# Self-attention on one Trainium2 core: five key tiles a step summed by accumulating transfers, one on TensorE, the narrow matmuls of a step in 9 blocks

## The chip, the cores and the metric

The kernel runs on one core of one Trainium2 chip. Its engines work side by side and are tied only by semaphores: TensorE (PE), VectorE (DVE), ScalarE (ACT), GpSimd (POOL) and SyncE (SP), which here only issues transfers. GpSimd issues transfers too, on a queue of its own. The metric is the device time of one execution in microseconds, lower is better.

## The reference

The program is a chain of transformer layers in fp32 on x of shape (2, 2048, 512): adaptive layer norm and cross attention, then a block with self-attention, cross attention and an mlp. The change touches only the self-attention, 16 heads of 32 channels over 2048 keys:

```python
def mha(q, k, v):
    B, Nq, C = q.shape
    d = C // H
    ...
    scores = jnp.einsum('bqhd,bkhd->bhqk', qh, kh) / jnp.sqrt(jnp.asarray(d, q.dtype))
    attn = jax.nn.softmax(scores, axis=-1)
    out = jnp.einsum('bhqk,bkhd->bqhd', attn, vh)
    return out.reshape(B, Nq, C)
...
qkv = h @ qkv_w + qkv_b
q, k, v = jnp.split(qkv, 3, axis=-1)
h = mha(q, k, v) @ self_o_w + self_o_b
```

## The kernel before

The stages follow one another: conditioning, a cross pass, a dense pass that makes q, k and v, `attention`, a second cross pass, and `mlp`. Each ends before the next begins.

`attention` makes 32 steps (`STEPS`): 2 batches, 4 groups of 4 heads (`GH`), 4 chunks of 512 queries (`W`). A step has for its 512 queries and 4 heads:

- 64 **score tiles** (`score_tile`, L1844), one for each of 16 key tiles and 4 heads: keys on the partitions, queries in the free dimension, into one of three PSUM banks `st`. ScalarE turns each into exponentials `e` (`exponential`, L1959). `e` has five slots (`ER`) of one key tile with its 4 heads, so key tile t+5 can be written only when all readers of tile t are done.
- 64 **peak units** (`score_unit`, L1822), the same scores with the queries on the partitions, into one of three banks `sm`. VectorE takes their largest value (`peak_of_unit`, L2003). They belong to the next step and the one after: the peaks must be known before a step's score tiles, since their negative is a row of q. `HEAD` = 21 says how many units of a step are done two steps ahead. When a step's 64 are done, VectorE makes `minus` (L2012, L2013), GpSimd the low part (`lower_parts`, L2077), TensorE turns them (`turn_peaks`, L1832) behind score tile `TURN` - 1 = 48, ScalarE copies them to `rows` (L1947), and SP spreads them into q by a transfer (`spread_rows`, L1763), which must be there before the next step's score tile 0.
- 16 **products** with v (`weigh`, L1857), 4 matmuls of 32 columns each into `acc[:, 0]`.
- The **sums of the exponentials** over the 16 key tiles, into `acc[:, 1]`. Ten tiles (`POOLED`) are added up by GpSimd into `esum` (`add`, L2070, nine adds). Four (`MOVED`) are summed by transfers that GpSimd issues into `esum_moved` (`move`): the first a copy (L2091), the others accumulating (L2094), each waiting for the one before it to land. Two (`SUMMED`) are multiplied by ones on TensorE (`add_up`, L1866). At the end `add_moved` (L1882) and `add_partial` (L1875) multiply `esum_moved` and `esum` by ones into the same sums.

A *unit* of narrow matmuls is what one call of `weigh`, `add_up`, `add_moved` or `add_partial` issues: four matmuls of 32 columns, eight in the records. A step has 20. TensorE's order is written out by hand: it goes through x = 0 to 63, and for each x issues score tile x, then the narrow units that `products` lists for x, then peak unit x. The narrow units stand in 11 *blocks*, at x = 0, 5, 10, 16, 22, 27, 33, 39, 44, 53, 59; the last units of a step come in the first blocks of the next. A score tile waits for the exponential that frees its bank (`bank_free`), three places back, and two back at the edge of a step, because a step has 65 places (64 tiles and the transposes). A peak unit waits for the peak three units back.

ScalarE copies `acc` out behind exponential `FETCH_AT` = 10 of the next step (`fetch_sums`, L1973). VectorE divides in three parts at units `DIVIDE_AT` (L2023, L2027, L2034), ScalarE spreads the inverse at `SPREAD_AT` = 42 (L1966), GpSimd scales (`scale`, L2083), and SP stores (L1772).

GpSimd's order within a step is also written out: move 0 before add 1, move 1 before add 3, move 2 and `lower_parts` before add 6, move 3 before add 8, `scale` before add 9. SP's order is: q for two steps ahead once score tile 63 of the step before is done (L1745, three transfers), in every fourth step k (L1753, three of 1 MB), then a wait for the sums of the step before and v (L1757), then the store, then the spread.

Of the kernel before, what the change touches and what calls it, by code (L numbers as in the profile page):

```python
# [16 lines left out]
HEADS, DH = 16, 32  # L17
# [1596 lines left out]
def attention(nc, d, name, q_in, k_in, v_in, o_out, keys, preload):  # L1614
# [10 lines left out]
    NKT = -(-keys // P)  # L1625
    KR = keys // NKT
# [9 lines left out]
    QR = 3  # L1636
    ER = 5

    POOLED = [0, 1, 3, 5, 7, 8, 9, 11, 13, 14]
    MOVED = [2, 6, 10, 12]  # L1640
    SUMMED = [4, 15]
    SUMMED_FIRST = [4, 15]
    ADDS = max(len(POOLED) - 1, 0)
    STEPS = B * GROUPS * CHUNKS
    BODY = STEPS
    TURN = 49
    HEAD = 21
    TILES = GH * NKT + 1
    RING = 3
    LATE = 1 if NKT > 1 else 2  # L1650
    DIVIDE_AT = (13, 23, 57)
    FETCH_AT, SPREAD_AT = 10, 42
    SETUP = 2 + KW % 2
    with nc.cleanup_on_exit(), ExitStack() as ctx:
        sb = lambda n, s, t=F32: ctx.enter_context(nc.sbuf_tensor(f"{name}_{n}", s, t))
# [3 lines left out]
        acc = ctx.enter_context(nc.psum_tensor(name + "_acc", [P, 2, W], F32))  # L1659
        ident = sb("ident", [P, P])  # L1660
        mask = sb("mask", [P, GH])
        ones = sb("ones", [P, DH])
# [4 lines left out]
        if POOLED:  # L1667
            esum = sb("esum", [P, GH, W])
            esum_moved = sb("esum_moved", [P, GH, W])
# [17 lines left out]
        e_moved, esum_read = sem("e_moved"), sem("esum_read")  # L1687
# [6 lines left out]
        def exists(i, j):  # L1694

            return not isinstance(i, int) or 0 <= BODY * i + j < STEPS
# [112 lines left out]
        def _(pe):  # L1809
# [61 lines left out]
            def add_partial(i, j):  # L1871

                pe.wait_ge(e_added, (BODY * i + j + 1) * ADDS)
                for h in range(GH):
                    mm = pe.matmul(acc[h * DH:(h + 1) * DH, 1], ones[0:KR], esum[:, h], start=False, stop=True, tile_position=(0, h * DH))  # L1875
                mm.then_inc(tile_used, 1)

            def add_moved(i, j):

                pe.wait_ge(e_moved, DMA * (BODY * i + j + 1) * len(MOVED))  # L1880
                for h in range(GH):
                    mm = pe.matmul(acc[h * DH:(h + 1) * DH, 1], ones[0:KR], esum_moved[:, h], start=False, stop=False, tile_position=(0, h * DH))  # L1882

            def products(i, j, x):

                if x == 0 and exists(i, j - 1):
                    weigh(i, j - 1, 13)
                    add_up(i, j - 1, 15)
                elif x == 5 and exists(i, j - 1):
                    weigh(i, j - 1, 14)  # L1890
                    weigh(i, j - 1, 15)
                elif x == 10 and exists(i, j - 1):
                    add_moved(i, j - 1)
                    add_partial(i, j - 1)
                elif x == 16 and exists(i, j):
                    weigh(i, j, 0)
                    weigh(i, j, 1)
                elif x == 22 and exists(i, j):
                    weigh(i, j, 2)
                elif x == 27 and exists(i, j):  # L1900
                    weigh(i, j, 3)
                    add_up(i, j, 4)
                elif x == 33 and exists(i, j):
                    weigh(i, j, 4)
                elif x == 39 and exists(i, j):
                    weigh(i, j, 5)
                    weigh(i, j, 6)
                elif x == 44 and exists(i, j):
                    weigh(i, j, 7)
                    weigh(i, j, 8)  # L1910
                    weigh(i, j, 9)
                elif x == 53 and exists(i, j):
                    weigh(i, j, 10)
                elif x == 59 and exists(i, j):
                    weigh(i, j, 11)
                    weigh(i, j, 12)

            def step(i, j):
                units = units_of_step(i, j)
# [140 lines left out]
        @block.gpsimd  # L2060
        def _(pool):
            def add(i, j, x):

                n, slot = BODY * i + j, lambda x: (j * NKT + POOLED[x]) % ER
                pool.wait_ge(score_read, number(i, j, place(POOLED[x], GH - 1)) + 3)
                if x > 1:
                    pool.wait_ge(e_added, n * ADDS + x - 1)
                elif exists(i, j - 1):
                    pool.wait_ge(tile_used, n * NKT + ER)
                pool.tensor_tensor(esum[:], e[:, slot(0)] if x == 1 else esum[:], e[:, slot(x)], ALU.add).then_inc(e_added, 1)  # L2070

            def lower_parts(i, j):

                n = BODY * i + j
                pool.wait_ge(neg_hi_ready, n + 1)
                pool.wait_ge(minus_ready, n + 1)
                pool.tensor_tensor(neg_part(1).bitcast(F32), minus[:], neg_part(0).bitcast(F32), ALU.subtract).then_inc(neg_lo_ready, 1)  # L2077

            def scale(i, j):
                n = BODY * i + j  # L2080
                pool.wait_ge(o_stored[j % 2], DMA * (BODY // 2 * i + j // 2 + 1))
                pool.wait_ge(divided, DIVIDES * (n + 1))
                pool.tensor_tensor(o[:, j % 2], sums[:, 0], inv_t[:, j % 2], ALU.mult).then_inc(scaled, 1)  # L2083

            def move(i, j, y):

                n, kt = BODY * i + j, MOVED[y]
                pool.wait_ge(score_read, number(i, j, place(kt, GH - 1)) + 3)
                if y == 0:
                    pool.wait_ge(tile_used, n * NKT + ER)  # L2090
                    pool.dma_start(esum_moved[:], e[:, (j * NKT + kt) % ER]).then_inc(e_moved, DMA)  # L2091
                else:
                    pool.wait_ge(e_moved, DMA * (n * len(MOVED) + y))
                    pool.dma_start(esum_moved[:], e[:, (j * NKT + kt) % ER], accum_op=ALU.add).then_inc(e_moved, DMA)  # L2094

            def step(i, j):
                for x in range(1, len(POOLED)):
                    if x == 1 and exists(i, j):
                        move(i, j, 0)
                    if x == 3 and exists(i, j):  # L2100
                        move(i, j, 1)
                    if x == 6 and exists(i, j):
                        move(i, j, 2)
                    if x == 8 and exists(i, j):
                        move(i, j, 3)
                    if x == 9 and exists(i, j - LATE):
                        scale(i, j - LATE)
                    if x == 6 and exists(i, j + 1):
                        lower_parts(i, j + 1)
                    if exists(i, j):  # L2110
                        add(i, j, x)

            pool.sem_inc(scaled, 2)
            pool.wait_ge(small_in, 2 * DMA)
            pool.tensor_copy(k[3 * DH:P, 1], mask[3 * DH:P].unsqueeze(2).to_broadcast([DH, GH, KC * KE])).then_inc(pool_set_up, 1)
            pool.wait_ge(pool_set_up, 1)
            lower_parts(0, 0)
            run(pool, step, LATE, LATE)


# [238 lines left out]
```

## Time and profile before

| | us |
|---|---|
| median of 3 runs | 4002.65 |
| lowest and highest | 3992.6, 4006.91 |
| the profiled execution, its own time | 4006.39 |
| its span in the trace | 4004.6 |
| attention: start of the first and of the last step | 945.2, 2587.7 |
| attention: last copy of the sums | 2649.0 |

The span is what the trace covers; the execution's own time is 1.8 us more. In a row of the timeline the first number is the start, the second the duration of the merged instructions, and x8 says how many they are; in brackets stands the idle time of the engine before them and what ended it. A matmul's recorded duration is longer than the distance to the next one, since they are pipelined: distances between starts are the measure.

### The profile page before, as it was taken

The numbers are of one execution on the slowest core, as the hardware profiler recorded it, in microseconds if no ns is written. First come the engines' busy times: TensorE is split into PE (matmuls) and PEld (weight loads), VectorE is DVE, ScalarE is ACT, GpSimd is POOL, SyncE is SP. The second block draws the span as 40 slices with busy tenths as digits, with TensorE's granted clock in tenths as the row PEclk, the third lists the DMA queues.
The fourth block names the chain that finished last, engine by engine and source line by source line (L and its number), as shares of the span: only waits on it lengthen the run. The fifth ranks groups of instructions, "written<-read, shape, count | busy, mean of one in ns | idle before, by whom it ended". The sixth has DMA issues, their size and how long they took to land. (4 is left out here: it accounts for less than half of the span.)

```text
span 4004.6 us, 50633 instructions
## 1 busy us (share of the span) xinstructions
PE 3667.1 (92%) x18828; PEld 2414.8 (60%) x18828; DVE 2261.2 (56%) x3958; ACT 1862.3 (47%) x3439; POOL 2175.1 (54%) x1075
## 2 busy tenths in 40 slices
PE   4799969979999999999999999958999959999998
PEld 2577748855555445454545455427777737888887
DVE  2466642228777777777777777515665634222222
ACT  1465651113666666666666666644665521111111
POOL 0356630004888888888888888864777542000000
PEclk8798889987999999999999999978999879999999
DMA  7566556764464645556464644444576551111110
GB/s 230 146 160 168 166 159 218 222 185 105 98 143 103 149 108 127 124 110 137 101 145 106 153 101 111 120 123 111 153 179 172 134 200 42 42 42 42 42 42 31
DMA packets 231940, 505.60 MB, mean 126 GB/s; under 512 B 38151, under 2 KB 55047, under 8 KB 211751
## 3 DMA queue, kind: packets, MB, share of 16 engines
q1 hardware_dynamic: 213287, 368.49, 33.6%
q0 software_dynamic: 18432, 134.23, 15.4%
q8 instruction: 131, 2.15, 0.2%
q14 instruction: 90, 0.74, 0.1%
HBM read 215.54 MB, written 144.51 MB: 90 GB/s over the span
## 5 line engine op out<-in xcount | busy, mean ns | idle before, releaser
L2003 DVE TENSOR_REDUCE a_peak<-a_sm 128x1 f32<-128x512 f32 x2048 | 1263.3, 680 | 396.0 <-PE a_sm L1822 394.7
L1959 ACT ACTIVATE a_e<-a_st 128x512 f32<-128x512 f32 x2048 | 1061.6, 604 | 539.1 <-PE a_st L1844 506.5
L2070 POOL TENSOR_TENSOR a_esum<-a_esum,a_e 128x2048 f32<-128x2048 f32 x256 | 1210.2, 4727 | 18.8 <-POOL a_esum L2070 0.4
L1822 PE MATMUL a_sm<-a_k,a_q 96*128 96x512 f32 x2048 | 883.9, 439 | 27.9 <-DMA a_k<-s_k 27.9
L1844 PE MATMUL a_st<-a_q,a_k 128*128 128x512 f32 x2048 | 827.2, 406 | 17.4 <-ACT a_e L1959 17.2
L1822 PEld LDWEIGHTS a_sm<-a_k,a_q 96*128 96x128 f32 x2048 | 394.8, 193 | 475.8 <-DVE a_peak L2003 337.5
L1857 PE MATMUL a_acc<-a_e,a_v 128*32 128x512 f32 x4096 | 505.7, 600 | 0.0
L1844 PEld LDWEIGHTS a_st<-a_q,a_k 128*128 128x128 f32 x2048 | 387.9, 190 | 137.3 <-ACT a_e L1959 62.8
L2220 PE MATMUL mlp_ph<-mlp_us,mlp_w_hi 128*128 128x512 f32 x1024 | 336.4, 391 | 33.0 <-DVE mlp_raw_lo L2269 33.0
L2262 ACT ACTIVATE mlp_gelu<-mlp_ph,mlp_b 128x512 f32<-128x512 f32 x128 | 88.1, 688 | 595.1 <-PE mlp_ph L2220 595.1
L2277 DVE CAST mlp_gs<-mlp_gelu 128x512 fp32r<-128x512 f32 x128 | 90.8, 709 | 459.0 <-ACT mlp_gelu L2262 459.0
L2300 POOL TENSOR_TENSOR mlp_x<-mlp_x,mlp_brow 128x2048 f32<-128x2048 f32 x8 | 36.9, 4616 | 569.7 <-DMA mlp_x<-s_x 569.4
L2235 PE MATMUL mlp_py<-mlp_w_hi,mlp_gs 128*128 128x512 f32 x1024 | 317.6, 391 | 16.9 <-DVE mlp_gs L2279 16.9
L1433 POOL TENSOR_TENSOR p_e<-p_e,p_inv 128x308 f32<-128x308 f32 x256 | 173.2, 708 | 175.5 <-DVE p_inv L1109 175.4
L2220 PEld LDWEIGHTS mlp_ph<-mlp_us,mlp_w_hi 128*128 128x128 f32 x1024 | 193.5, 189 | 73.7 <-issue 33.4
L1857 PEld LDWEIGHTS a_acc<-a_e,a_v 128*32 128x32 f32 x4096 | 100.4, 108 | 219.6 <-ACT a_e L1959 124.7
L2235 PEld LDWEIGHTS mlp_py<-mlp_w_hi,mlp_gs 128*128 128x128 f32 x1024 | 191.8, 188 | 61.3 <-issue 16.3
L589 PE MATMUL p_sm<-p_ks,p_qs 96*128 96x78 f32 x1024 | 171.5, 310 | 51.0 <-DMA p_qs<-s_q 30.1
L589 PEld LDWEIGHTS p_sm<-p_ks,p_qs 96*128 96x128 f32 x1024 | 157.1, 222 | 82.8 <-DMA p_qs<-s_q 28.3
L2220 PE MATMUL mlp_ph<-mlp_us,mlp_raw_lo 128*128 128x512 f32 x512 | 200.1, 391 | 0.0
L2235 PE MATMUL mlp_py<-mlp_raw_lo,mlp_gs 128*128 128x512 f32 x512 | 199.9, 390 | 0.0
L1094 DVE TENSOR_REDUCE p_top<-p_sm 128x4 f32<-128x308 f32 x256 | 118.4, 465 | 142.5 <-PE p_sm L589 140.5
(155 smaller groups left out, 5255.1 us busy)
## 6 DMA issues: line engine op xcount, KB each, us to landing
a_esum_moved<-a_e POOLq DMA_DIRECT2D x128, 1024.0 KB, 7.3
p_qs<-s_q SPq DMA_DIRECT2D x192, 256.0 KB, 5.7
s_q<-p_qo SPq DMA_DIRECT2D x64, 512.0 KB, 7.2
a_q<-s_q SPq DMA_DIRECT2D x96, 256.0 KB, 6.8
a_k<-s_k SPq DMA_DIRECT2D x24, 1024.0 KB, 15.7
s_x<-p_x SPq DMA_DIRECT2D x16, 1024.0 KB, 4.4
s_u<-p_ut_hi SPq DMA_DIRECT2D x64, 256.0 KB, 5.8
s_u<-p_ut_lo SPq DMA_DIRECT2D x64, 256.0 KB, 6.3
```

What stands on the lines that cost most here:

```text
L589: mm = pe.matmul(sm[:, unit % 2, h * KE:(h + 1) * KE], qs[0:3 * DH, g % 2, h, qt * P:(qt + 1) * P], ks[0:3 * DH, b, g * GH + h], start=Tru ...
L1094: dve.tensor_reduce(top[:, unit % 4], src, AX.X, ALU.max).then_inc(top_done, 1)
L1433: pool.tensor_tensor(e[:, number % 2, qt, :, 0:S], e[:, number % 2, qt, :, 0:S], inv[:, number % 2, qt].unsqueeze(2).to_broadcast([P, GH, ...
L1822: mm = pe.matmul(sm[:, bank_of_unit(j, u), x * KE:(x + 1) * KE], q[0:3 * DH, j % QR, h, qt * P:(qt + 1) * P], k[0:3 * DH, g % 2, h, kc * K ...
L1844: pe.matmul(st[0:KR, place(kt, h) % RING], k[:, g % 2, h, kt * P:kt * P + KR], q[:, j % QR, h], start=True, stop=True).then_inc(score_done, 1)
L1857: mm = pe.matmul(acc[rows, 0], v[0:KR, g % 2, kt, rows], e[0:KR, (j * NKT + kt) % ER, h], start=(kt == 0), stop=(kt == NKT - 1), tile_posi ...
L1959: act.activation(e[0:KR, (j * NKT + kt) % ER, h], st[0:KR, place(kt, h) % RING], ACT.Exp, scale=SCALE).then_inc(score_read, 1)
L2003: dve.tensor_reduce(dst, src, AX.X, ALU.max).then_inc(unit_read, 1)
L2070: pool.tensor_tensor(esum[:], e[:, slot(0)] if x == 1 else esum[:], e[:, slot(x)], ALU.add).then_inc(e_added, 1)
L2220: mm = pe.matmul(ph[:, m % 4], w1[pw][:, t, m * P:(m + 1) * P], us[:, b, pm, t], start=(t == 0 and s == 0), stop=(t == KT - 1 and s == 2))
L2235: mm = pe.matmul(py[:, tt], gs[:, m % 2, pw, tt * P:(tt + 1) * P], w2[pm][:, m], start=(m == 0 and s == 0), stop=(m == HT - 1 and s == 2))
L2277: dve.tensor_copy(gs[:, m % 2, 0], gelu[:, m % 2]).then_inc(g_hi, 1)
```

## The change

The tiles are shared out anew: ten on GpSimd as before, but others, five instead of four by transfers, and one instead of two on TensorE. A step has 19 narrow units in 9 blocks, at x = 6, 10, 15, 20, 28, 34, 42, 49, 63. `add_partial` comes before `add_moved`, which now stands at x = 15 and closes the sums; a new semaphore count (`esum_read`) tells GpSimd when `esum` has been read, so that its first add of a step waits for `add_partial` alone, and move 0, now behind add 1, waits for `add_moved`. `add_up` of tile 15 stands in the block at x = 63 of the same step. `TURN`, `HEAD`, `DIVIDE_AT`, `FETCH_AT`, `SPREAD_AT` and the places of the moves and of `lower_parts` among the adds are set anew.

```diff
-    POOLED = [0, 1, 3, 5, 7, 8, 9, 11, 13, 14]
-    MOVED = [2, 6, 10, 12]
-    SUMMED = [4, 15]
-    SUMMED_FIRST = [4, 15]
+    POOLED = [0, 1, 3, 4, 6, 7, 9, 10, 12, 13]
+    MOVED = [2, 5, 8, 11, 14]
+    SUMMED = [15]
+    SUMMED_FIRST = [15]
...
-    TURN = 49
-    HEAD = 21
+    TURN = 54
+    HEAD = 16
...
-    DIVIDE_AT = (13, 23, 57)
-    FETCH_AT, SPREAD_AT = 10, 42
+    DIVIDE_AT = (26, 36, 61)
+    FETCH_AT, SPREAD_AT = 15, 40
...
 # add_partial
-                    mm = pe.matmul(acc[h * DH:(h + 1) * DH, 1], ones[0:KR], esum[:, h], start=False, stop=True, tile_position=(0, h * DH))
-                mm.then_inc(tile_used, 1)
+                    mm = pe.matmul(acc[h * DH:(h + 1) * DH, 1], ones[0:KR], esum[:, h], start=False, stop=False, tile_position=(0, h * DH))
+                mm.then_inc(esum_read, 1)
 # add_moved
-                    mm = pe.matmul(acc[h * DH:(h + 1) * DH, 1], ones[0:KR], esum_moved[:, h], start=False, stop=False, tile_position=(0, h * DH))
+                    mm = pe.matmul(acc[h * DH:(h + 1) * DH, 1], ones[0:KR], esum_moved[:, h], start=False, stop=True, tile_position=(0, h * DH))
+                mm.then_inc(tile_used, 1)
 # products
-                if x == 0 and exists(i, j - 1):
-                    weigh(i, j - 1, 13)
-                    add_up(i, j - 1, 15)
-                elif x == 5 and exists(i, j - 1):
+                if x == 6 and exists(i, j - 1):
                     weigh(i, j - 1, 14)
+                elif x == 10 and exists(i, j - 1):
+                    add_partial(i, j - 1)
                     weigh(i, j - 1, 15)
-                elif x == 10 and exists(i, j - 1):
+                elif x == 15 and exists(i, j - 1):
                     add_moved(i, j - 1)
-                    add_partial(i, j - 1)
-                elif x == 16 and exists(i, j):
+                elif x == 20 and exists(i, j):
                     weigh(i, j, 0)
                     weigh(i, j, 1)
-                elif x == 22 and exists(i, j):
+                elif x == 28 and exists(i, j):
                     weigh(i, j, 2)
-                elif x == 27 and exists(i, j):
                     weigh(i, j, 3)
-                    add_up(i, j, 4)
-                elif x == 33 and exists(i, j):
                     weigh(i, j, 4)
-                elif x == 39 and exists(i, j):
+                elif x == 34 and exists(i, j):
                     weigh(i, j, 5)
+                elif x == 42 and exists(i, j):
                     weigh(i, j, 6)
-                elif x == 44 and exists(i, j):
                     weigh(i, j, 7)
+                elif x == 49 and exists(i, j):
                     weigh(i, j, 8)
                     weigh(i, j, 9)
-                elif x == 53 and exists(i, j):
                     weigh(i, j, 10)
-                elif x == 59 and exists(i, j):
+                elif x == 63 and exists(i, j):
                     weigh(i, j, 11)
+                    add_up(i, j, 15)
                     weigh(i, j, 12)
+                    weigh(i, j, 13)
...
 # GpSimd: add
                 elif exists(i, j - 1):
-                    pool.wait_ge(tile_used, n * NKT + ER)
+                    pool.wait_ge(esum_read, n)
...
 # GpSimd: step
                 for x in range(1, len(POOLED)):
-                    if x == 1 and exists(i, j):
+                    if x == 2 and exists(i, j):
                         move(i, j, 0)
-                    if x == 3 and exists(i, j):
+                    if x == 4 and exists(i, j):
                         move(i, j, 1)
                     if x == 6 and exists(i, j):
                         move(i, j, 2)
                     if x == 8 and exists(i, j):
                         move(i, j, 3)
+                    if x == 9 and exists(i, j):
+                        move(i, j, 4)
                     if x == 9 and exists(i, j - LATE):
                         scale(i, j - LATE)
-                    if x == 6 and exists(i, j + 1):
+                    if x == 7 and exists(i, j + 1):
                         lower_parts(i, j + 1)
```

## Rows read from the trace of the kernel before

**Rows 1.** the page: the span, and GpSimd's DMA queue (packets, MB, share)

```profile
span 4004.6 us, 50633 instructions
...
q0 software_dynamic: 18432, 134.23, 15.4%
```

**Rows 2.** a stretch: us; PE, PEld, DVE, ACT, POOL busy; TensorE's clock; DMA share, GB/s

```profile
1207.00:1841.00 634.00, 626.13 (x3475) 317.12 (x3476) 487.56 (x821) 417.13 (x798) 544.85 (x179) 1.00 0.56 124
```

**Rows 3.** timeline of TensorE, one step

```profile
2130.86 0.40 PE L1844 MATMUL a_st<-a_q,a_k 128*128 128x512 f32 x1
...
2131.44 0.39 PE L1844 MATMUL a_st<-a_q,a_k 128*128 128x512 f32 x1
...
2133.09 0.40 PE L1844 MATMUL a_st<-a_q,a_k 128*128 128x512 f32 x1
...
2133.56 0.40 PE L1844 MATMUL a_st<-a_q,a_k 128*128 128x512 f32 x1
...
2148.58 0.39 PE L1844 MATMUL a_st<-a_q,a_k 128*128 128x512 f32 x1
...
2148.90 2.78 PE L1857 MATMUL a_acc<-a_e,a_v 128*32 128x512 f32 x24
...
2151.95 0.40 PE L1844 MATMUL a_st<-a_q,a_k 128*128 128x512 f32 x1
...
2156.38 0.40 PE L1844 MATMUL a_st<-a_q,a_k 128*128 128x512 f32 x1
...
2164.46 0.40 PE L1844 MATMUL a_st<-a_q,a_k 128*128 128x512 f32 x1
...
2165.28 0.47 PE L1844 MATMUL a_st<-a_q,a_k 128*128 128x512 f32 x1 [0.19 <-ACT a_e L1959]
...
2218.02 0.47 PE L1844 MATMUL a_st<-a_q,a_k 128*128 128x512 f32 x1 [0.19 <-ACT a_e L1959]
```

**Rows 4.** timeline of VectorE, the run of nine units

```profile
2152.15 5.47 DVE L2003 TENSOR_REDUCE a_peak<-a_sm 128x1 f32<-128x512 f32 x9 [1.73 <-PE a_sm L1822]
```

**Rows 5.** timeline of GpSimd, one step

```profile
2126.18 4.61 POOL L2070 TENSOR_TENSOR a_esum<-a_e 128x2048 f32<-128x2048 f32 x1
...
2136.43 0.88 POOL L2094 DMA_DIRECT2D a_esum_moved<-a_e  x1 [0.91 <-ACT a_e L1959]
...
2137.06 14.35 POOL L2070 TENSOR_TENSOR a_esum<-a_esum,a_e 128x2048 f32<-128x2048 f32 x3
...
2151.36 0.84 POOL L2094 DMA_DIRECT2D a_esum_moved<-a_e  x1
...
2168.10 4.85 POOL L2070 TENSOR_TENSOR a_esum<-a_esum,a_e 128x2048 f32<-128x2048 f32 x1
```

**Rows 6.** the accumulating transfers (L2094), issue to landing

```profile
DMA to landing us min/median/max: 6.9/7.5/9.7
```

**Rows 7.** DMA queues, 2163 to 2168 us: packets, MB, share

```profile
q0 software_dynamic: 124, 1.02, 113.0%
...
a_q<-s_q SPq DMA_DIRECT2D x3, 256.0 KB, 6.6
```

**Rows 8.** the spread of the rows (L1763), the one at 2155

```profile
L1763 SPq DMA_DIRECT2D a_q<-a_rows x1: 605/605/605, 2155.1 to 2155.1; - x1
...
DMA to landing us min/median/max: 4.8/4.8/4.8
```

**Rows 9.** timeline of TensorE, tile 0 around a load step

```profile
2005.02 0.47 PE L1844 MATMUL a_st<-a_q,a_k 128*128 128x512 f32 x1 [0.19 <-ACT a_e L1959]
...
2059.71 0.47 PE L1844 MATMUL a_st<-a_q,a_k 128*128 128x512 f32 x1 [0.19 <-ACT a_e L1959]
```

**Rows 10.** DMA issues from 2017 us on: KB each, us to landing

```profile
a_esum_moved<-a_e POOLq DMA_DIRECT2D x1, 1024.0 KB, 13.6
```

**Rows 11.** DMA queues, 2018 to 2024 us, the load step

```profile
q1 hardware_dynamic: 175, 1.30, 103.3%
```

**Rows 12.** timeline of ScalarE in the load step

```profile
2031.64 3.04 ACT L1959 ACTIVATE a_e<-a_st 128x512 f32<-128x512 f32 x6 [3.04 <-DMA a_esum_moved<-a_e]
```

## Prediction

> **What bounds the kernel now.** The page gives the span, 4004.6 us [rows 1], and names the mlp as the end of its chain; the change touches only the attention stage, so I read that stage. The table by stretches shows it: in 634 us TensorE is busy for 626, VectorE for 488, ScalarE for 417, GpSimd for 545, at a granted clock of 1.00, which is the 2.4 GHz level [rows 2]. TensorE is therefore the bound, GpSimd the next, and what matters is how TensorE's own order of work is paced. That is read from its timeline. I measure from the start of one score matmul (L1844) to the next; position x of a step is its score tile x, and I call 0 the start of tile 0 of a step.
>
> [Rows 3] give: a step takes 2218.02-2165.28 = 52.74 us. A plain pair (score tile, peak unit) takes 0.47 (2133.09 to 2133.56). A gap with a one-unit block of narrow matmuls in it takes 1.65 (2131.44 to 2133.09), with three units 3.37 (2148.58 to 2151.95), so a unit is 0.86, and a block costs 0.32 beside its units and the pair. Two-unit gaps are then 2.51, four-unit gaps 4.23.
>
> Now the sum of a step before: 53 plain gaps x 0.47 = 24.9, three one-unit blocks, seven two-unit, one three-unit: 25.9. Together 50.8; the other 1.9 us are waits. Three of them can be seen. In a run of six units between blocks the last gap is 0.58 and not 0.47 (2130.86 to 2131.44): +0.11. In the run of nine (x=44 to 53) the eight gaps 2151.95 to 2156.38 take 4.43 and not 3.76: +0.67, of which the transposes are a part. At the step's edge tile 63 to tile 0 takes 0.82: +0.35, ended by ScalarE, because 65 places a step are not a multiple of three banks and tile 0 needs the exponential of tile 62. Five runs of six, the nine and the edge make 1.6; 0.35 stays spread over small waits.
>
> The cause of the waits in runs is VectorE: nine peaks took 5.47 us without a gap, 0.61 each [rows 4], against 0.47 for a pair. Three score banks let TensorE be about two units ahead; from the sixth unit of a run on it goes at VectorE's pace, 0.14 more a unit. A block lets VectorE catch up.
>
> **The change, part by part.**
> Blocks: one unit less (an add_up, L1866) and two blocks less. After, a step is 55 plain gaps, 25.85, and 3x1.65 + 3x2.51 + 2x3.37 + 4.23 = 23.45: 49.3 against 50.8, -1.50 a step.
>
> Runs: blocks at 6, 10, 15, 20, 28, 34, 42, 49, 63 leave runs of 7, 4, 5, 5, 8, 6, 8, 7 and 14 units, where before none but the nine was over six. With 0.11 for the sixth unit and 0.14 for each behind it: 0.25 + 0.39 + 0.11 + 0.39 + 0.25 + 1.23 = 2.62, plus 0.14 for the transposes in the run of 14 (0.67 less the 0.53 that the rule gives for nine), plus the unexplained 0.35. The edge wait of 0.35 goes: a four-unit block stands between tiles 63 and 0. Waits after: 3.1 against 1.9. **A step becomes 52.4, -0.3 us.** The long runs give back nearly all that the blocks save. Could ScalarE bound the run of 14? No: its exponential is shorter than a peak, the stage's busy sums say so (417 against 488).
>
> GpSimd: it now starts behind add_partial at x=10 and no longer at tile 2. x=10 comes at 6x0.47+0.25+1.65+3x0.47 = 6.1, so add_partial is read by 7.5 and the first add starts at 7.7. Before, from the first add (2126.18) to the end of the ninth (2172.95) were 46.8 us with 0.9 idle at 2136.43; adds go at 4.78 (14.35 for three), a transfer's issue takes 0.6 of its time (2136.43 to 2137.06) [rows 5]. After: 46.8-0.9, and five issues in place of three, +1.2: 47.1. New wait: the fourth transfer goes at 7.7+7x4.78+3x0.61+0.2 = 43.2, the fifth is due one add later, 48.6, but must wait for the fourth to land: 7.5 in the median, 9.7 at most [rows 6]; with 7.9 it goes at 51.1, a wait of 2.5. Behind it on GpSimd are scale and the last add, which ends at 57.5, that is 5.1 into the next step. add_partial asks for it at 6.45. It is covered with 1.3 to spare; each us beyond that would cost 31 us. What it costs now: nothing.
>
> Fifth transfer, issued at 51.1 (-1.3): tile 14's slot is wanted by the exponential of tile 3; TensorE stops at x=15 (10.5) unless that slot is free by 9.9, and add_moved stands there too. Landing 7.9 later gives 6.6: hidden, and at 6.9 or 9.7 too; only transfers of SP that go first can change that, below.
>
> Row spread (a_q from a_rows, SP): due before tile 0. In five us of a summing transfer 124 packets of GpSimd's queue went and none of SP's, though three q loads were issued there [rows 7]. So the spread of now, issued at 2155.15, landed 4.8 later [rows 8], 8.6 after the transfer of 2151.36. After, the fourth transfer at 43.2 stands just ahead of it: landed 51.8, tile 0 is at 52.4. Hidden with 0.6 to spare, but it is a floor: a step can't fall below about 51.8.
>
> Steps in which k and v are loaded (every fourth, six with a step before them): now 2059.71-2005.02 = 54.69, +2.0 [rows 9]. The plain transfer of tile 2 landed after 13.6 there [rows 10], as SP's 1.30 MB went first [rows 11]; ScalarE waited 3.04 for it [rows 12]. After, it is issued at 12.5 (behind the first add), lands at 26.1, and TensorE wants exponential 28 by 24.6: with that exponential's 0.6 and the relay a wait of some 2.3, where the whole excess is now 2.0. Loads start 3.4 earlier (tile 63 starts four units sooner before the edge), but the fifth transfer takes those 5 us of the engines. GpSimd then waits 4 us for that landing before its next transfer, and comes to add_partial later by 1 or so than its 1.3 allow for. I take 3.3 in place of 2.0: +8 over six. Bounds: 0 (-12 in all) and 8 (+36).
>
> Ends: HEAD moves five units from the prologue, where VectorE paces them (5x0.61 = 3), into step 30, where TensorE has room (+1); step 0 has one unit more of its own (+1): -1; in the last step the ninth add now ends at 60.4 (its step began at 2165.28-52.74 = 2112.54, the first add at 13.6, and 46.8 more), and will at 57.5, with the fifth transfer landed at 59.0: -2 for what follows the sums.
>
> How far the DMA engines favour one queue: they stayed with GpSimd's for a whole summing transfer, and with SP's for six us, while the other had work [rows 7, 11]. The Trainium skill, DMA: Bandwidth & Descriptors, section on queues, rings and completion order, says that each DMA engine takes turns between its queues and changes only after a whole packet of some 9 to 17 descriptors. The page's 18432 records for 128 transfers [rows 1] are 144 each, nine on every engine, so by that rule a transfer of a tile would go through in one turn, and would itself wait for one turn of SP's at most: rival (c) below would then cost some +8 and not the +35 that the plain copy's long landing leads to. The chances below don't lean on it.
>
> **Sum.** 30 whole steps x -0.31 = -9.3; ends -3; load steps +8: -4.3. The profiled execution is 4006.39, 1.8 beside its span, and 3.7 above the median. 4006.4-4.3 = 4002.1; for the median, 4002.65-4.3 = 3998.4, say 3998. Within 0.3% (12 us) counts as no change: about what a measurement can tell.
>
> **Rivals.**
> (a) The long runs cost little: VectorE's lag is swallowed. For: 1.2 us of the sum rests on one run of 14, and the longest of before was nine. Against: nine contiguous peaks. Then the row spread is the floor, 51.8: 30 x -0.94 = -28, -3, +8: 4002.65-23 = 3980. Faster. 0.20.
> (b) The load steps lose their stall, as k starts earlier and the transfer of tile 2 is later wanted by a block of three: 3998-8-12 = 3978 (its eight gone, the two a step of now as well). Faster. 0.12.
> (c) Slower: the fifth transfer goes behind k. k is issued at the same time as it, and 1.30 MB of SP's went in six us, 4.6 per MB [rows 11]. One MB ahead: landing 12.5 after issue, 1.3 late (it decides from 11.2 on); two ahead: 17.1, 5.9 late, x6 = +35: 4033. For: the 13.6 of the plain copy [rows 10]. Against: it is issued while the short q loads pass. 0.16.
> (d) GpSimd becomes the bound: with landings of 9.7 the last add is 0.5 late each step: +16: 4014. 0.08.
> (e) The forecast: 0.44; it lies within 12 us of before but for its edges (0.04 faster, 0.01 slower).
>
> Faster 0.36, same 0.39, slower 0.25. Range: 3970 takes in (a) and (b), 4032 (d) and most of (c) short of its end.
>
> **What would show it.** Tile 50 to tile 63 taking 7.5 on TensorE's timeline, with VectorE contiguous for 14 peaks of 0.61; the gap 63 to 0 of 4.2; steps of 52.4; GpSimd waiting about 2.5 for the landing before its fifth transfer and idle 2.6 until add_partial has been read; no wait of TensorE before L1875 or L1882; tile 0 not held by the spread; load steps of 55 to 56. I am wrong if the run of 14 has waits other than VectorE's, if the period is one set by GpSimd or by the spread, or if add_moved waits in load steps.

## The result: 1.9% slower

The changed kernel takes 4072.3 us in the median of 4 runs (4068.9 to 4080.4), the kernel before 3997.7 in its runs beside it; the ratio is 1.0189, 95% interval 1.0168 to 1.0210. The forecast was 3998, with a range of 3970 to 4032.

The profiled execution took 4068.9 us. Its timeline of TensorE, an ordinary step from tile 0 to tile 0 (2167.51 to 2220.95), with the run of 14 units in it, answers to [rows 3]:

```profile
2167.51 0.50 PE L1844 MATMUL a_st<-a_q,a_k 128*128 128x512 f32 x1 [1.12 <-DMA a_q<-a_rows]
...
2204.95 0.39 PE L1844 MATMUL a_st<-a_q,a_k 128*128 128x512 f32 x1
2205.27 2.78 PE L1857 MATMUL a_acc<-a_e,a_v 128*32 128x512 f32 x24
...
2208.33 0.40 PE L1844 MATMUL a_st<-a_q,a_k 128*128 128x512 f32 x1
...
2215.58 0.40 PE L1844 MATMUL a_st<-a_q,a_k 128*128 128x512 f32 x1
2215.91 1.06 PE L1857 MATMUL a_acc<-a_e,a_v 128*32 128x512 f32 x8
2216.80 1.04 PE L1866 MATMUL a_acc<-a_e,a_ones 128*32 128x512 f32 x8
2217.66 1.90 PE L1857 MATMUL a_acc<-a_e,a_v 128*32 128x512 f32 x16
2219.49 0.50 PE L1822 MATMUL a_sm<-a_k,a_q 96*128 96x512 f32 x1
2220.95 0.50 PE L1844 MATMUL a_st<-a_q,a_k 128*128 128x512 f32 x1 [0.96 <-DMA a_q<-a_rows]
```

The step takes 53.44, not 52.4. Tile 49 to tile 50 is 3.38 and tile 50 to tile 63 is 7.25: block and run are as worked out (3.37 and 7.5). But tile 63 to tile 0 is 5.37 where 4.23 was due, and the bracket names the row spread. VectorE in the same run, answering to [rows 4]: 13 peaks in one piece, 0.61 each.

```profile
2208.53 7.87 DVE L2001 TENSOR_REDUCE a_peak<-a_sm 128x1 f32<-128x512 f32 x13 [1.73 <-PE a_sm L1822]
```

GpSimd and SP around the spread, from their timelines (L1763 is the spread), with the landing of this spread and of the fourth transfer, each as the view of its line gives it; they answer to [rows 5, 8]:

```profile
2206.41 4.58 POOL L2068 TENSOR_TENSOR a_esum<-a_esum,a_e 128x2048 f32<-128x2048 f32 x1
2210.93 0.85 POOL L2092 DMA_DIRECT2D a_esum_moved<-a_e  x1
...
2220.73 0.88 POOL L2092 DMA_DIRECT2D a_esum_moved<-a_e  x1 [4.30 <-DMA a_esum_moved<-a_e]
```

```profile
2211.52 0.60 SPq L1763 DMA_DIRECT2D a_q<-a_rows  x1
```

```profile
L1763 SPq DMA_DIRECT2D a_q<-a_rows x1: 605/605/605, 2211.5 to 2211.5; - x1
...
DMA to landing us min/median/max: 9.4/9.4/9.4
```

```profile
L2092 POOL DMA_DIRECT2D a_esum_moved<-a_e x1: 848/848/848, 2210.9 to 2210.9; - x1
...
DMA to landing us min/median/max: 9.3/9.3/9.3
```

The fourth transfer is issued 43.4 into the step (43.2 was forecast), the spread 0.6 behind it. Neither lands in its old time: 9.3 for the one and 9.4 for the other, where such a transfer took 7.5 and the spread 4.8. The spread lands at 2220.9, and tile 0 starts at once.

The DMA queues from 2211 to 2218 us, answering to [rows 7], and then from 2218 to 2221 us show why. First GpSimd's queue moves its 1.05 MB and SP's, on which the spread was issued at 2211.52, only 0.11; by the packets in the trace SP's first one starts 4.0 us after the spread's issue, 1.3 where the spread is issued 6 us behind a transfer (e3). Then SP's moves almost alone, with the rest of the spread and the first q loads behind it.

```profile
q0 software_dynamic: 135, 1.05, 80.4%
q1 hardware_dynamic: 56, 0.11, 7.5%
```

```profile
q1 hardware_dynamic: 319, 0.59, 83.6%
q0 software_dynamic: 9, 0.00, 0.2%
```

The load steps are the larger part. TensorE's timeline, tile 0 of one and of the next step (answers to [rows 9]) and between them where it stood; then ScalarE, GpSimd and SP:

```profile
2050.19 0.50 PE L1844 MATMUL a_st<-a_q,a_k 128*128 128x512 f32 x1 [1.10 <-DMA a_q<-a_rows]
...
2060.61 0.40 PE L1822 MATMUL a_sm<-a_k,a_q 96*128 96x512 f32 x1
2068.33 0.79 PE L1844 MATMUL a_st<-a_q,a_k 128*128 128x512 f32 x1 [7.32 <-ACT a_e L1957]
2069.05 1.94 PE L1882 MATMUL a_acc<-a_esum_moved,a_ones 128*32 128x512 f32 x8
...
2113.92 0.50 PE L1844 MATMUL a_st<-a_q,a_k 128*128 128x512 f32 x1 [1.14 <-DMA a_q<-a_rows]
```

```profile
2067.68 2.08 ACT L1957 ACTIVATE a_e<-a_st 128x512 f32<-128x512 f32 x4 [7.69 <-DMA a_esum_moved<-a_e]
```

```profile
2049.96 0.88 POOL L2092 DMA_DIRECT2D a_esum_moved<-a_e  x1 [4.41 <-DMA a_esum_moved<-a_e]
```

```profile
2049.05 1.72 SPq L1753 DMA_DIRECT2D a_k<-s_k  x3
```

k's three loads are issued from 2049.05 on, the fifth transfer at 2049.96, 0.9 behind the first of them. It landed after 17.6 (the view of L2092 at that issue), at 2067.6. Until then tile 14's slot isn't free, ScalarE waits 7.7 for it, and TensorE 7.3 at tile 15. This step took 63.7.

The queues in the two halves of that stretch, 2049 to 2056 us and 2056 to 2064 us, answer to [rows 11]. In the first only SP's queue moves, in the second both share:

```profile
q1 hardware_dynamic: 452, 1.56, 105.1%
```

```profile
q0 software_dynamic: 111, 0.91, 55.1%
q1 hardware_dynamic: 129, 0.93, 46.1%
```

**Adding up.** From tile 0 of step 0 to tile 0 of step 28 the stage took 1557.5 us, before 1485.8: +71.7. The six load steps of it took 62.5 to 65.1 each, in place of 54.3 to 55.4: +51.6. The other 22 took 53.5 on average, in place of 52.6: +20, of which 3.2 are in step 0 (52.5 against 49.3). The last scale of the stage started at 2730.1 and not 2652.7, +77.4. What is missing to that is mostly the end: from tile 0 of the last step (2659.7, before 2588.8; the 2587.7 in the table of times before is tile 63 of the step before) to the last scale it took 70.4 in place of 63.9, +6.5. There TensorE waited for GpSimd's last add, 3.0 later in its step than before, and behind it came three units at 1.7 each where before came one. Changed kernel, then kernel before:

```profile
2720.97 1.94 PE L1875 MATMUL a_acc<-a_esum,a_ones 128*32 128x512 f32 x8 [5.44 <-POOL a_esum L2068]
```

```profile
2647.01 1.94 PE L1875 MATMUL a_acc<-a_esum,a_ones 128*32 128x512 f32 x8 [2.44 <-POOL a_esum L2070]
```

(The stages behind attention were 15 us shorter in this execution, 1337.0 against 1351.9. Their code is the same in both kernels; see the last section.)

### The profile page after: what moved, and what is told of

Its sections match the earlier page's. It is cut to its first block and busy times, and to the rows that moved or that the text cites. A ratio compares the mean times of both kernels' runs of the same rounds, so it can differ in the third digit from the quotient of the medians.

```text
span 4067.1 us, 50185 instructions
## 1 busy us (share of the span) xinstructions
PE 3663.3 (90%) x18572; PEld 2397.7 (59%) x18572; DVE 2258.0 (56%) x3958; ACT 1876.2 (46%) x3439; POOL 2205.5 (54%) x1107
## 5 line engine op out<-in xcount | busy, mean ns | idle before, releaser
L1957 ACT ACTIVATE a_e<-a_st 128x512 f32<-128x512 f32 x2048 | 1073.7, 605 | 624.3 <-PE a_st L1844 493.8
L1822 PE MATMUL a_sm<-a_k,a_q 96*128 96x512 f32 x2048 | 907.2, 450 | 28.3 <-DMA a_k<-s_k 28.3
L1857 PEld LDWEIGHTS a_acc<-a_e,a_v 128*32 128x32 f32 x4096 | 110.6, 109 | 252.5 <-issue 183.4
L2235 PEld LDWEIGHTS mlp_py<-mlp_w_hi,mlp_gs 128*128 128x128 f32 x1024 | 191.8, 188 | 61.2 <-issue 16.1
L589 PE MATMUL p_sm<-p_ks,p_qs 96*128 96x78 f32 x1024 | 168.3, 307 | 52.7 <-DMA p_qs<-s_q 31.3
```

The costliest lines, as they stand in the source:

```text
L589: mm = pe.matmul(sm[:, unit % 2, h * KE:(h + 1) * KE], qs[0:3 * DH, g % 2, h, qt * P:(qt + 1) * P], ks[0:3 * DH, b, g * GH + h], start=Tru ...
L1822: mm = pe.matmul(sm[:, bank_of_unit(j, u), x * KE:(x + 1) * KE], q[0:3 * DH, j % QR, h, qt * P:(qt + 1) * P], k[0:3 * DH, g % 2, h, kc * K ...
L1857: mm = pe.matmul(acc[rows, 0], v[0:KR, g % 2, kt, rows], e[0:KR, (j * NKT + kt) % ER, h], start=(kt == 0), stop=(kt == NKT - 1), tile_posi ...
L1957: act.activation(e[0:KR, (j * NKT + kt) % ER, h], st[0:KR, place(kt, h) % RING], ACT.Exp, scale=SCALE).then_inc(score_read, 1)
L2235: mm = pe.matmul(py[:, tt], gs[:, m % 2, pw, tt * P:(tt + 1) * P], w2[pm][:, m], start=(m == 0 and s == 0), stop=(m == HT - 1 and s == 2))
```

## The experiments

Theory A: the order of the blocks costs what was worked out, and two collisions on the DMA engines make the loss, the fifth transfer with k in the load steps and the row spread with the fourth transfer in every step. The rivals: GpSimd's chain is the bound (B, C), TensorE's order is slower by itself (D), VectorE is behind by as much wherever the blocks stand (E), five transfers are too many anywhere (F). For each run the table gives the median, the ratio to the kernel before on the same chip with its 95% interval, the start of the last scale in its trace (2652.7 before, 2730.1 changed), and a typical gap from tile 0 to tile 0 of ordinary and of load steps.

| run | median us | ratio (interval) | last scale | ordinary | load |
|---|---|---|---|---|---|
| e1 changed, loads apart | 4011.9 | 1.0028 (1.0013-1.0043) | 2672.4 | 53.5 | 53.5 |
| e2 changed, spread earlier | 4028.0 | 1.0072 (1.0045-1.0099) | 2693.6 | 52.6 | 56.5-62.3 |
| e3 both | 3987.0 | 0.9976 (0.9962-0.9990) | 2643.8 | 52.6 | 52.6 |
| e4 before, loads apart | 3980.7 | 0.9959 (0.9946-0.9972) | 2640.9 | 52.7 | 52.7 |
| e5 as e3, long run split | 3979.2 | 0.9952 (0.9938-0.9965) | 2636.0 | 52.3 | 52.3 |
| e6 before, fifth transfer, loads apart | 3979.7 | 0.9956 (0.9943-0.9969) | 2642.4 | 52.4 | 52.4-55 |
| e7 before, fifth transfer | 4040.6 | 1.0107 (1.0092-1.0122) | 2709.7 | 51.9 | 64.1-66.1 |
| e8 changed, no fifth transfer | 4024.6 | 1.0076 (1.0059-1.0093) | 2678.1 | 54.3 | 53.0 (first 54.6) |
| e9 as e6, loads placed earlier | 3969.8 | 0.9936 (0.9922-0.9949) | 2625.6 | 51.9-53.7 | 51.9 |
| e10 changed, k behind the fifth | 4059.6 | 1.0155 (1.0138-1.0172) | 2716.5 | 53.5 | 59.3-62.0 |

### e1: the loads of k and v taken apart

```diff
-                if j % CHUNKS == 0 and exists(i, j + CHUNKS):
-                    load_k(i, j // CHUNKS + 1)
...
-                    load_v(i, j // CHUNKS + 1)
                 if exists(i, j - LATE - 1):
                     store_o(i, j - LATE - 1)
+                if exists(i, (j // CHUNKS + 1) * CHUNKS):
+                    sp.wait_ge(score_done, number(i, j, 22) + 1)
+                    sp.sem_inc(passed, 1)
+                    if j % CHUNKS < 3:
+                        load_k(i, j // CHUNKS + 1, (j % CHUNKS,))
+                    else:
+                        load_v(i, j // CHUNKS + 1)
```

> The changed kernel with the loads of k taken apart: one of its three 1 MB parts in each of the first three steps of a group, v in the fourth, each issued behind score tile 22, where no other transfer is due. Theory A (the loss has two parts: the fifth transfer shares the DMA engines with k in every fourth step, about 9.4 us each time, and the row spread is late in every step): the six long steps of 62 to 65 us fall to the 53.5 of the others, 6 x 9.4 = -56, so about 4016 us; the wait before tile 0 stays at some 1.1 us. Rival B (the long steps are long for another cause, GpSimd's own chain): they stay above 60 and the time within 10 us of 4072. If the parts of k now disturb other transfers, three steps in four grow by 1 to 2 us and the time is 4035 to 4060.

Measured 4011.9: the long steps are gone and the others are as they were, with the gap from tile 63 to tile 0 at 5.5. Theory A stands, B falls. Taking the loads apart gave back 60 us. The loss was 75; but some 12 of the 60 are the 2 us a load step that the kernel before loses too.

### e2: peaks, transposes and spread five tiles earlier

```diff
-    TURN = 54
-    HEAD = 16
+    TURN = 49
+    HEAD = 22
...
-                    if x == 7 and exists(i, j + 1):
+                    if x == 6 and exists(i, j + 1):
                         lower_parts(i, j + 1)
```

> The changed kernel with TURN 49, HEAD 22 and lower_parts before add 6: peaks, transposes and the row spread come five tiles earlier, before the fourth transfer is issued and not just behind it; TensorE's blocks and the five transfers stay. Theory A: the spread lands in some 4.8 us, about 7 us before tile 0, the gap from tile 63 to tile 0 falls from 5.5 to 4.2, ordinary steps from 53.5 to 52.2, and the fourth transfer lands sooner too; load steps keep their 9 us: 31 x -1.3 = -40, about 4032. Rival C (GpSimd is the real bound and the wait for the spread only hides it): the wait moves to add_partial or to the transposes and ordinary steps stay above 53: 4060 to 4072. The prologue has six more units: +3.

Measured 4028.0, the gap at the edge 4.24, and the spread landed after 3.3 in the median (9.5 in the changed kernel). Ordinary steps are 52.6 and not 52.2: the earlier transposes stand in front of a block, where the gap at x=48 is 0.96 (0.66 in the changed kernel), and runs of six and seven wait a little more. The load steps lost 3.2 each as well, which I had not expected: the edit also brings the fifth transfer 2.6 earlier, at 50.8 into the step. In two of them it was issued 0.4 and 0.5 ahead of k's first load and took 16.2 and 13.9; in the other four, 0.2 to 0.8 behind it, 16.9 to 18.6. GpSimd is not the bound: in e3, which has the same order, it waits for TensorE once a step, before its first add, 2.5 us in the step shown. Rival C falls. That wait in GpSimd's timeline of e3:

```profile
2163.85 4.59 POOL L2069 TENSOR_TENSOR a_esum<-a_e 128x2048 f32<-128x2048 f32 x1 [2.50 <-PE a_acc L1876]
```

### e3: both; e4: the loads alone, in the kernel before

e3 is e1 and e2 together; e4 puts the diff of e1 into the kernel before.

> Both edits together. Theory A: steps of 52.2 throughout, 31 x 52.2 and no long steps: 4072 - 56 - 40 = 3976, 22 us below the kernel before, which is what blocks and runs alone were worked out to give (-0.3 to -0.5 a step) plus the stalls of the load steps of before (-12). Rival D (the order with a run of 14 units is itself slower than that of before): ordinary steps above 52.7 and a time of 3990 or more.

> The kernel before with the same taking apart of the k and v loads and nothing else. Theory A: its load steps lose their 2.0 us each and step 0 to 4 as well: about -12, 3986. If the parts of k meet its transfers of tiles 6 or 2, the gain is lost: 3995 to 4005. It also says how much of the third run's gain belongs to the loads and how much to the order.

e3 came to 3987.0, 11 more than expected. By the medians both edits give 85, and one alone 60 and 44: 19 more in sum. The load steps account for these 19, since e2 had shortened the six of them by 19 in its trace, and e1 gives the same back. The 11 above what was expected are the ordinary steps, 52.6 and not 52.2. With both collisions gone the change is 0.2% faster than the kernel before. But e4, which has nothing of the change, came to 3980.7, and the two intervals overlap. So the new sharing of tiles and the order of blocks bring nothing that can be measured: 52.6 a step against 52.7. What e3 has over the kernel before is the load steps, which lost their 2 us. Rival D's sign, steps above 52.7 and 3990 or more, didn't come; but it is right in so far as the order isn't better.

### e5: the run of 14 split

```diff
-                elif x == 63 and exists(i, j):
+                elif x == 56 and exists(i, j):
                     weigh(i, j, 11)
-                    add_up(i, j, 15)
                     weigh(i, j, 12)
+                elif x == 63 and exists(i, j):
                     weigh(i, j, 13)
+                    add_up(i, j, 15)
```

> The third run's kernel (loads taken apart, spread earlier) with the four-unit block at x=63 split in two: tiles 11 and 12 at x=56, tile 13 and the sum of tile 15 at x=63, so the run of 14 units becomes two of 7. Theory A (VectorE's 0.61 a peak paces the long run, 0.13 for each unit from the sixth on): the nine gaps of 0.60 between tiles 54 and 63 shrink to 0.47 but for one or two, -0.9 to -1.0; one block more costs 0.32; steps go from 52.6 to about 52.0, -18 over 31: 3969. Rival E (VectorE would be behind by as much anyway, its work per step being the same): the waits reappear behind the new block and steps are 52.6 to 52.9: 3987 to 3996.

Measured 3979.2, steps 52.3 against 52.6. The waits did not come back, so rival E falls, but the gain is 0.3 and not 0.6, and the time is 10 above what was expected. I had counted the expectation wrong: of the nine gaps of 0.60 in the run of 14 four stay, two in each run of seven; five times 0.13 less a block's 0.32 is 0.33, which is what came.

### e6 and e7: the fifth transfer alone, in the kernel before

```diff
-    MOVED = [2, 6, 10, 12]
-    SUMMED = [4, 15]
-    SUMMED_FIRST = [4, 15]
+    MOVED = [2, 4, 6, 10, 12]
+    SUMMED = [15]
+    SUMMED_FIRST = [15]
...
-                    add_up(i, j, 4)
...
-                    if x == 3 and exists(i, j):
+                    if x == 2 and exists(i, j):
                         move(i, j, 1)
-                    if x == 6 and exists(i, j):
+                    if x == 4 and exists(i, j):
                         move(i, j, 2)
-                    if x == 8 and exists(i, j):
+                    if x == 6 and exists(i, j):
                         move(i, j, 3)
+                    if x == 8 and exists(i, j):
+                        move(i, j, 4)
```

e7 is this in the kernel before; e6 has the loads apart as well, as in e1.

> The fourth run's kernel (the kernel before with the loads taken apart) with one thing of the change alone: a fifth tile (4) summed by a transfer, in place of its add_up at x=27, the transfers spread over GpSimd's adds at x = 1, 2, 4, 6, 8, blocks and all else as before. Theory A (a fifth transfer costs nothing where no load and no spread stands beside it; what hurts in the change is its place at the end of the step): steps 52.7 - 0.86 = 51.9, 31 x -0.86 = -27: about 3954. Rival F (five transfers with 7 us of landing each are too many for GpSimd's chain or the engines, wherever they stand): steps stay at 52.7 or grow, 3981 or more.

> The same fifth transfer in the kernel before with its k and v loads where they were, 4 MB at the start of every fourth step. Theory A: ordinary steps 51.9; in load steps the copy of tile 2 lands after 13.6 us as before and the second transfer, due 5 us behind it, waits on GpSimd for 8, so that the chain is 4 us later still: load steps 54 to 58. 3998 - 27 + 6 x (0 to 3) = 3971 to 3990. Rival F: 3998 or more.

e7's ordinary steps are 51.9, as expected: in the middle of the step a fifth transfer is free and its unit of 0.86 is gained. The total is 4040.6, far from the 3971 to 3990 expected, by its load steps: 65 us. GpSimd's and TensorE's timelines of e7 in one of them:

```profile
2062.17 0.60 POOL L2090 DMA_DIRECT2D a_esum_moved<-a_e  x1 [4.21 <-ACT a_e L1958]
2062.78 4.59 POOL L2069 TENSOR_TENSOR a_esum<-a_e 128x2048 f32<-128x2048 f32 x1
2079.47 0.89 POOL L2093 DMA_DIRECT2D a_esum_moved<-a_e  x1 [12.09 <-DMA a_esum_moved<-a_e]
```

```profile
2079.65 0.80 PE L1844 MATMUL a_st<-a_q,a_k 128*128 128x512 f32 x1 [4.85 <-ACT a_e L1958]
2085.68 0.50 PE L1844 MATMUL a_st<-a_q,a_k 128*128 128x512 f32 x1 [0.90 <-ACT a_e L1958]
2088.56 0.49 PE L1844 MATMUL a_st<-a_q,a_k 128*128 128x512 f32 x1 [0.68 <-ACT a_e L1958]
2100.94 1.11 PE L1832 MATMUL a_st<-a_ident,a_neg 128*128 128x128 f32 x4 [2.04 <-POOL a_neg L2076]
```

The second transfer waits 12.1 us for the first to land, its own slot and GpSimd's next adds come late, and TensorE stands at four places and not at one. I had put the copy's landing at 13.6 and the second transfer's wait at 8; in the six load steps the copy took 16.3 to 17.3, though it and k are issued at nearly the same places of the step as before. Why it took 3 us longer is not shown.

By its total e7 lies where rival F wanted it (3998 or more), but its ordinary steps don't grow, as F says they must. e6 came to 3979.7 and not 3954: its parts of k, issued behind score tile 22, met the transfer of tile 4, which took 10.3 in the median (7.0 in e7), GpSimd was late with the low part of the peaks, and the gap at x=48 was 1.36 where it is 0.84. It is no faster than e4, so only e9 below settles F.

### e8: the changed kernel without its fifth transfer

```diff
-    MOVED = [2, 5, 8, 11, 14]
-    SUMMED = [15]
-    SUMMED_FIRST = [15]
+    MOVED = [2, 5, 8, 11]
+    SUMMED = [15, 14]
+    SUMMED_FIRST = [15, 14]
...
                 if x == 6 and exists(i, j - 1):
+                    add_up(i, j - 1, 14)
                     weigh(i, j - 1, 14)
...
-                    if x == 9 and exists(i, j):
-                        move(i, j, 4)
```

> The changed kernel with the sum of tile 14 back on TensorE (add_up in the block at x=6) and no fifth transfer; loads, spread and order as changed. Theory A: the six long steps lose the 9.4 us that were spent waiting for the fifth transfer beside k and keep at most the 2 us of the kernel before; the unit costs 0.86; the spread stays late by 1.1 or so, since it is the fourth transfer that stands before it, but the step's floor is set by that, so that the unit is partly hidden: steps of 53.5 to 54.3, in all 4072 - 56 + (0 to 27) = 4016 to 4043. Rival B (GpSimd's chain or k itself makes the long steps long): they stay above 60 and the time above 4072.

Measured 4024.6. Five of the six load steps, with k still loaded in one piece, are 53.0, shorter than the ordinary ones of 54.3; the first is 54.6. Rival B falls once more: neither k alone nor the fifth transfer alone (e1) makes steps of 63. The unit put back costs 0.8 of its 0.86 in the ordinary steps; hardly any of it is hidden.

The edge of these steps also tells what delays the spread. In the ordinary steps but the first and the last the gap there is still 4.5 to 6.1. In the five load steps of 53.0 it is 4.2: there GpSimd comes later by a little, and the fourth transfer is issued 0.0 to 0.7 behind the spread and not 0.6 ahead of it. SP's and GpSimd's issues at the end of a load step and of the next one, and the landing of the two spreads (3.5 and 9.4):

```profile
2067.72 0.60 SPq L1763 DMA_DIRECT2D a_q<-a_rows  x1
2068.32 0.86 POOL L2093 DMA_DIRECT2D a_esum_moved<-a_e  x1
...
2120.52 0.87 POOL L2093 DMA_DIRECT2D a_esum_moved<-a_e  x1
2121.14 0.61 SPq L1763 DMA_DIRECT2D a_q<-a_rows  x1
```

```profile
DMA to landing us min/median/max: 3.5/3.5/3.5
...
DMA to landing us min/median/max: 9.4/9.4/9.4
```

So the spread's lateness is the fourth transfer's doing, and it hangs on which of the two is issued first. The q loads that SP issues 4.6 behind the spread are not the cause: the last spread but one has none behind it and still took 9.4 in the changed kernel and 9.1 here.

### e9: the loads placed where no transfer is due

As e6, without the wait for score tile 22: each part goes right behind the store.

```diff
-                    sp.wait_ge(score_done, number(i, j, 22) + 1)
-                    sp.sem_inc(passed, 1)
```

> The sixth run's kernel (kernel before, five transfers, loads of k and v in four parts) with each part issued right behind the store of the step, before the copy of tile 2 is due, and not behind score tile 22, where it met the transfer of tile 4. Theory A: the transposes no longer wait for GpSimd (the 0.5 at x=48 that the sixth run had in most steps is gone), ordinary steps are the 51.9 that the seventh run had: 31 x (51.9 - 52.4) = -16 against 3980, about 3962, some 36 below the kernel before. If the part now holds up the copy of tile 2, the wait is only moved: 3975 to 3990.

Measured 3969.8, 8 more than expected, ratio 0.9936: faster than both kernels, with load steps of 51.9 and about half of the others too; the rest are 52 to 53.7, where the transposes still wait (x=48: 0.84 in the median, 1.08 in the mean). Against e4 the last scale comes 15 us earlier, so rival F falls. It holds one idea of the change, the fifth transfer, put in the middle of the step.

### e10: k behind the fifth transfer

```diff
+                    if exists(i, j - 1):
+                        sp.wait_ge(e_moved, DMA * (BODY * i + j) * len(MOVED))
+                        sp.sem_inc(passed, 1)
                     load_k(i, j // CHUNKS + 1)
```

> The changed kernel; in load steps SP waits until the fifth transfer of the step before has landed, and only then issues the 3 MB of k. Theory A (k ahead of the fifth transfer on the shared engines is what holds tile 14's slot): no wait at x=14 and 15 any more, but the copy of tile 2 then meets k, which starts some 8 us later than now, and waits longer: load steps from 63 to 56 to 60, 4072 - 6 x (3 to 7) = 4030 to 4054. Rival B (k's loads cost load steps the same 9 us wherever they stand, as 3 MB need the engines for 16 us): 4066 to 4076, with the wait moved to score tile 28.

Measured 4059.6, between what A and B wanted. The wait at x=14 and 15 is gone (0.47 and 1.66 there, as in e1) and has moved to tile 2's copy, as ScalarE's timeline of e10 shows in one load step:

```profile
2072.99 2.08 ACT L1960 ACTIVATE a_e<-a_st 128x512 f32<-128x512 f32 x4 [8.88 <-DMA a_esum_moved<-a_e]
```

The copy now took 15.5 to 18.1. Load steps are still 59 to 62, 7.4 over an ordinary step where the changed kernel has 9.9. So the order of k and the fifth transfer gives back a quarter; in both orders, and in e7, 3 MB in one piece held up the summing transfer that was due beside it.

## Why the prediction was wrong

- **Blocks and runs: right.** One unit and two blocks less, and the long runs at VectorE's 0.61, were the right sizes: 3.38 for the three-unit block, 7.25 for the run (7.5 forecast), 4.24 for the four-unit gap with the spread out of the way (e2, e3; 4.23 forecast). Take the 1.3 of the late spread off an ordinary step and 52.2 is left, 52.4 forecast. e5 shows the long run's cost by taking half of it away.
- **GpSimd's chain: right in place, one wait too small.** The fourth transfer at 43.4 (43.2) and a wait before the fifth, but of 4.3 and not 2.5, since the fourth landed after 9.3. The 1.3 to spare was used up: the gap at x=10 is 2.65, 0.14 over a plain two-unit gap. Rival (d) had this landing nearly right, 9.7; it priced 0.5 a step, and 0.14 came.
- **The step that failed, first: "the fourth transfer at 43.2 stands just ahead of it: landed 51.8 ... Hidden with 0.6 to spare".** I carried over 8.6 us from the transfer's issue to the spread's landing, a distance from a step in which the spread came 3.8 behind the transfer. Now it comes 0.6 behind, its packets start 4.0 after its issue and not 2.6, and the transfer lands later too: 10.0 from the one's issue to the other's landing. It lands 53.4 into the step. 0.6 to spare became 1.1 to 1.3 late in nearly every step. The 22 steps without loads, forecast 0.3 shorter, are 0.9 longer; e2 gives 20 back there.
- **The step that failed, second and larger: the load steps, "I take 3.3".** That is their excess over an ordinary step; it measured 9.9, and against the kernel before the six cost 51.6 in place of some +6 (the +8, less 0.3 a step). What held them was the fifth transfer, landing after 17 to 19.5 behind k; e1, without k beside it, gives 60 us back.

  Rival (c), the fifth transfer behind k, was named at the right place. Its price comes out nearly: 3.3 + 5.9 = 9.2 against 9.9. That is in part luck. It had the transfer issued 1.3 before tile 0; it was 0.2 before, so that it was late from 10.1 us after its issue on and not from 11.2. And the landing of 17.1 (17.6 measured) was made of two whole MB that go first; in the trace 1.56 MB go first and then both queues share the engines. The wait of 2.3 at exponential 28, for the copy of tile 2, didn't come: nearly the whole excess stands at x=14 to 17.

  I gave the rival 0.16, on the ground that the fifth transfer is issued while short q loads pass. k's first load was issued 0.9 before it.

  The Trainium skill, DMA: Bandwidth & Descriptors, section on queues, rings and completion order, says that a DMA engine takes turns between its queues, packet by packet, and by it this rival came to a small +8. The trace agrees for the second part only: from 2056 to 2064 us the two queues moved side by side, but from 2049 to 2056 SP's alone. By its packets the transfer starts 6.0 to 6.5 us after its issue in the load steps and 1.4 to 1.5 in the others; whether it missed its turns in that time or wasn't ready for them is not shown.
- **Rival (b)** was wrong in sign: k's earlier start didn't relieve the load steps, it brought k onto the fifth transfer. e10 shows that turning the two round leaves most of the stall.
- **Rival (a)** was wrong: the long runs cost what VectorE's rate says.
- **Ends: -3 forecast, and a loss came.** The stage started 1.4 earlier, but step 0 took 3.2 more and the end 6.5 more. The last add was to end 57.5 into the last step and ended at 61.2, and the two units that now stand behind add_partial were not counted.

## What to carry to other kernels

A transfer has two prices: the issue, and the landing beside whatever else is on the engines when it moves, and the landing can turn on which of two is issued half a microsecond sooner (e8: 3.5 or 9.4). Before adding one, lay all queues' transfers over one period and check each deadline with the landing that it has in company, not the one it has alone; a distance between two transfers holds only for the spacing at which it was read. A large load that comes every few steps is worth taking apart before anything else is moved: here that alone gave 0.4% (e4), and only then did the fifth transfer pay (e9, 0.6% in all).

Removing blocks between two alternating streams saves their switch cost, and gives it back where the slower of the engines behind the streams can no longer catch up: count the longest run, not the number of blocks.

## What the runs showed of the hardware that was not expected

- A summing transfer of 1 MB on GpSimd's queue landed after 7.5 us in the median of the kernel before. A 256 KB spread of SP's landed after 4.8 when issued 3.8 behind one, 9.4 when issued 0.6 behind one, and 3.3 when issued 6.0 behind one (e2, e3) or up to 0.7 ahead of one (e8: 3.3 to 3.7). The transfer issued 0.6 ahead of the spread took 9.3 itself.
- The same transfer issued 0.9 us behind the first of three 1 MB loads took 17.6. For 6 us nothing of it moved.
- The stages behind attention took 1333 to 1352 us over the twelve profiled executions, with the same code. In the cross pass TensorE's granted clock was 0.87 in the one of the kernel before (2653 to 3240 us) and 0.89 in the changed kernel's (2730 to 3305 us), and the pass 587 and 575 us long. A change in one stage is therefore read better from that stage's end, here the last scale, than from one execution's span:

```profile
2653.00:3240.00 587.00, 503.83 (x2688) 397.82 (x2688) 329.44 (x659) 300.99 (x551) 351.00 (x317) 0.87 0.57 149
```

```profile
2730.00:3305.00 575.00, 491.78 (x2688) 387.73 (x2688) 328.37 (x659) 302.53 (x553) 351.66 (x318) 0.89 0.59 152
```
